# A decoder block: moments of two normalisations moved to ScalarE, two residuals to TensorE, value products paired, weights of the second stage loaded early

## What is computed

```python
x = x + self_attention(layernorm(x))                  # 3 live branches of 16 heads, windows as masks
q = split(layernorm(x) @ Wq.T + bq)                   # 16 heads of 32
k, v = split(ctx @ Wk.T + bk), split(ctx @ Wv.T + bv) # ctx: 722 keys per batch
scores = einsum('bhqd,bhkd->bhqk', q, k) / sqrt(32)
top, idx = top_k(scores, 32)                          # the 32 highest of 722, for each row
x = x + (softmax(top) @ v[idx]) @ Wo.T + bo
x = x + real(ifft(fft(layernorm(x)) @ w)) + bias      # folded into one 512x512 matrix M
```

## Time and profile before

| | us |
|---|---|
| device time, median of 3 runs (2321.08 to 2322.66) | 2322.45 |
| device time of the profiled execution | 2323.47 |
| its span | 2321.6 |
| DVE busy | 1950.9 (84%) |
| PE busy | 2076.8 (89%) |
| PEld busy | 1627.4 (70%) |
| ACT busy | 1266.3 (55%) |
| POOL busy | 1277.2 (55%) |

### The profile page before, as it was taken

How to read it: one execution, slowest core, us unless ns; L and a number is a source line. 1 busy time by engine, 2 the same in 40 slices (tenths; PEclk the granted TensorE clock), 3 DMA queues, 4 the chain that set the end, 5 groups by cost and what they waited for, 6 DMA issues and landing times. The chain is left out here.

```text
span 2321.6 us, 50944 instructions
## 1 busy us (share of the span) xinstructions
PE 2076.8 (89%) x19760; PEld 1627.4 (70%) x19760; DVE 1950.9 (84%) x3662; ACT 1266.3 (55%) x2464; POOL 1277.2 (55%) x1473
## 2 busy tenths in 40 slices
PE   2899999999957889999999999999999999999966
PEld 1566666666644778787787787887878778788754
DVE  4757676676722499999999999999999999999995
ACT  4333333333312476766666666766666766666652
POOL 2555646465641465656556656556556655665642
PEclk9999999999968899999999999999999999999977
DMA  5000000000036100000001000010000000100000
GB/s 190 12 16 20 16 23 13 23 13 26 9 82 191 30 19 13 30 26 21 18 21 38 19 20 25 13 37 18 20 26 23 28 18 21 37 18 21 8 1 11
DMA packets 41501, 70.42 MB, mean 30 GB/s; under 512 B 4639, under 2 KB 21167, under 8 KB 41261
## 3 DMA queue, kind: packets, MB, share of 16 engines
q1 hardware_dynamic: 35868, 56.31, 7.8%
q0 software_dynamic: 3632, 7.58, 1.4%
q10 hardware_dynamic: 1760, 3.28, 0.5%
HBM read 60.54 MB, written 9.86 MB: 30 GB/s over the span
## 5 line engine op out<-in xcount | busy, mean ns | idle before, releaser
L1384 DVE MATCH_REPLACE8 ca_W<-ca_top,ca_W 128x722 f32<-128x722 f32 (+1 forms) x624 | 553.1, 892 | 0.0
L1372 DVE MAX8 ca_top<-ca_W 128x8 f32<-128x722 f32 (+1 forms) x624 | 536.8, 897 | 2.2
L950 POOL TENSOR_TENSOR ca_S<-ca_S,ca_W 128x722 f32<-128x722 f32 (+1 forms) x208 | 358.6, 1743 | 270.5 <-ACT ca_W L1229 270.5
L1229 ACT ACTIVATE ca_W<-ca_W,ca_shift 128x722 f32<-128x722 f32 (+1 forms) x208 | 185.6, 892 | 83.8 <-DVE ca_W L1384 83.7
L927 POOL TENSOR_TENSOR ca_KL<-ca_K,ca_KH 128x384 fp32r<-128x384 f32 (+1 forms) x128 | 122.7, 959 | 191.5 <-ACT ca_KH L1221 189.7
L1251 ACT ACTIVATE ca_PT<-ca_pT 128x768 f32<-128x768 f32 (+1 forms) x208 | 163.4, 786 | 105.4 <-PE ca_pT L1091 105.1
L88 PE MATMUL ca_pS<-ca_KH,ca_QH 128*128 128x362 f32 (+1 forms) x384 | 149.7, 390 | 79.1 <-ACT ca_S L1246 77.4
L1124 PE MATMUL ca_pO<-ca_PT,ca_V 128*32 128x56 f32 (+5 forms) x4608 | 216.9, 225 | 0.0
L1239 ACT ACTIVATE ca_S<-ca_S,ca_shift 128x722 f32<-128x722 f32 (+1 forms) x208 | 175.8, 891 | 60.8 <-POOL ca_shift L942 60.5
L1362 DVE MAX8 ca_top<-ca_S 128x8 f32<-128x722 f32 (+1 forms) x208 | 178.9, 897 | 28.2 <-ACT ca_S L1246 27.7
L88 PE MATMUL ca_pF<-ca_cH,ca_WkH 128*128 128x338 f32 (+1 forms) x512 | 191.8, 375 | 10.2 <-POOL ca_cL L935 9.5
(11 more groups left out here) (212 smaller groups left out, 5178.0 us busy)
## 6 DMA issues: line engine op xcount, KB each, us to landing
ca_raw<-in_ctxT SPq DMA_DIRECT2D x32, 384.0 KB, 4.2
ca_raw<-in_ctxT SPq DMA_DIRECT2D x32, 338.0 KB, 3.0
sa_xin<-in_x SPq DMA_DIRECT2D x16, 200.0 KB
sa_xres<-in_x SPq DMA_DIRECT2D x16, 200.0 KB
x_scratch<-sa_x SPq DMA_DIRECT2D x16, 200.0 KB
x_scratch<-y_scratch POOLq DMA_DIRECT2D x16, 200.0 KB, 15.1
ca_xin<-x_scratch SPq DMA_DIRECT2D x16, 200.0 KB
ca_x<-x_scratch SPq DMA_DIRECT2D x16, 200.0 KB
```

Source lines behind the costliest of these rows:

```text
L950: pool.tensor_tensor(S[k][rows, :], S[k][rows, :], W[r][rows, :], ALU.subtract).then_inc(p_ready, 1)
L1229: act.activation(W[r][rows, :], W[r][rows, :], ACT.Exp, bias=shift[rows, r:r + 1], scale=SCALE).then_inc(f_ready, 1)
L1372: n_of[t.i] = order.mark(dve.max(top[r][rows, 8 * k:8 * k + 8], W[r][rows, :]))
L1384: ins = dve.match_replace(W[r][rows, :], eight, W[r][rows, :], REMOVED)
```

## The change

Six edits, in one version:

1. **Early loads.** A class `Early` places the fold matrices, the DFT matrix, the signs and the eight pieces of Wk and Wv over memory of the self program that its last batch no longer reads. SyncE issues their 29 transfers in that batch, behind a wait for the last product that reads it.
2. **Another order for batch 0.** `FIRST_PLAN` and `FIRST_SLICES` take all K slices first, and the V slices in step 0; the first score of batch 0 stands behind five slices. A second pair of context buffers (`cH0`, `cL0`) holds the second half. VectorE, idle there, makes the low parts of context and queries. The bias product (L1159 before) goes into batch 0.
3. **Six score buffers for seven**, taken round by step over the batches; the `settle` instructions (empty ones) are gone.
4. **Paired value products.** Instead of one tile's products after each transpose, the products of both tiles of a step stand at its end, from two `PT` buffers; `strip_order` orders the four blocks by how far each strip has come.
5. **Moments on ScalarE.** Total and sum of squares come from ACTIVATEs with an accumulated output, mean and scale from four small GpSimd operations, and an ACTIVATE does the scaling. BN_STATS, BN_AGGR, the epsilon and both scalings leave VectorE.
6. **Residuals on TensorE.** `x2` is multiplied with the identity into `pX` after the product, so that ScalarE only copies.

```diff
+class Early:
...
+            self.fold = {n: sb("fold_" + n, [128, CC, D]) for n in FOLDS}
+            self.dft, self.signs = sb("dft", [128, CC, D]), sb("signs", [128, CC, 4, 2])
+            self.staged = [sb(f"staged{u}", [128, D]) for u in range(2 * CC)]
...
+                    if cur and not nxt:
+                        sp.wait_ge(qk_mm, QB * B)
+                        early.load(sp)
...
-    RING, SLOTS = 4, 7
+    RING, SLOTS = 4, 6
+    FIRST_SLICES = sorted(SLICES, key=lambda x: x[1])
+    FIRST_PLAN = [([8, 9, 10], [11, 12, 13]), ([], [0, 1]), ([2], [3]), ([4], []), ([], []), ([], []), ([5, 6, 7], [])]
...
+            def mean(done):
+                pool.tensor_scalar(away[:, :], total[:, :], -1.0 / D, None, ALU.mult).then_inc(done, 1)
+
+            def scales(done):
+                order.after(order.mark(pool.tensor_scalar(rstd[:, :], squares[:, :], 1.0 / D, LN_EPS, ALU.mult, ALU.add)))
+                order.after(order.mark(pool.tensor_tensor(rstd[:, :], rstd[:, :], minus_half[:, :], ALU.pow)))
+                pool.tensor_tensor(center[:, :], away[:, :], rstd[:, :], ALU.mult).then_inc(done, 1)
...
+            def strip_order(sizes):
+                at, order = {}, []
+                for n, (strip, columns) in enumerate(sizes):
+                    for k in range(KC):
+                        order.append((at.get(strip, 0), n, k))
+                        at[strip] = at.get(strip, 0) + columns
+                return [(n, k) for _, n, k in sorted(order)]
...
-                        for c in range(CC):
-                            ins = pe.matmul(pX[0:T, :], ctxT[:, c, :], WoT[:, c, :], start=c == 0, stop=c == CC - 1)
-                        ins.then_inc(y_mm, 1)
+                        for c in range(CC):
+                            pe.matmul(pX[0:T, :], ctxT[:, c, :], WoT[:, c, :], start=c == 0, stop=False)
+                        pe.wait_ge(xb_ready, b.count(1, 0))
+                        pe.matmul(pX[0:T, :], ident[0:T, 0:T], x2[:, :], start=False, stop=True).then_inc(y_mm, 1)
...
-                        values(*old[1])
+                        values(*old)
...
+                    if s == 3 and prev:
+                        act.wait_ge(mean2_ready, b.count(1, 0))
+                        act.activation(pX[0:T, :], x2[:, :], ACT.Square, bias=away[:, 0:1],
+                                       accum_out=squares[:, 0:1]).then_inc(squares2_ready, 1)
...
+                    if s == 2 and prev:
+                        act.wait_ge(y_mm, b.count(1, 0))
+                        act.activation(x2[:, :], pX[0:T, :], ACT.Copy, accum_out=total[:, 0:1]).then_inc(x2_ready, 1)
...
-                        if k == 0 and s == 3 and prev:
-                            dve.wait_ge(y_mm, b.count(1, 0))
-                            dve.wait_ge(xb_ready, b.count(1, 0))
-                            dve.tensor_tensor(x2[:, :], pX[0:T, :], x2[:, :], ALU.add).then_inc(x2_ready, 1)
...
-                            row_stats(dve, order, x2[:, :], stats[:, :], mv[:, :], var2_ready)
```

413 lines of the change are left out of this document (239 added, 174 removed).

## The result

| | before | after |
|---|---|---|
| device time, median of 4 runs each | 2321.76 us (2319.46 to 2322.66) | 2236.81 us (2235.66 to 2242.63) |
| ratio, 95% interval | | 0.9641 (0.9622 to 0.9659) |
| profiled execution, its span | 2323.5, 2321.6 us | 2236.97, 2235.2 us |

A forecast was written before the change was run, and what follows sets the result against it. VectorE's full list was taken to bound the batches, TensorE 6% behind. Gains 72.8 + 2.6 + 47 - 1 - 3 = 118.4 us gave 2204 us, 5.1% faster; own range 2192 to 2214, with rivals 2190 to 2238.

The forecast's parts named there:

- VectorE's list: VectorE in the batches: all extras but one product leave its work, 89.0 + 0.3 us a batch for 94.5.
- The pairs: TensorE's paired value products: 1.3 us a pair for 2.05, saving 4.5 us a batch, hidden and not in the sum.
- The identity matmuls: Both residual matmuls on TensorE: 0.9 us each, 1.8 a batch, taken as hidden behind VectorE.
- The early loads: Start of the cross program: with the data there, the second product ends at 714, 21.6 us earlier.
- The end: After the last pick: residual matmuls and moments cost more, pairing saves about 1; sum 3 us more, 34 us in all.
- 85.9: TensorE's predicted time a batch in us, 88.6 + 1.8 - 4.5, under VectorE's 89.3.
- The step that failed: VectorE in the batches: period 89.3 us for 94.5 if nothing else limits; 14 x 5.2 = 72.8 us gained.
- second rival: TensorE becomes the bound if pairing saves nothing: 90.4 us a batch, 2220 us, up to 2250; chance 8%.
- first rival: A new wait in the batches, a score late for VectorE: 1 to 2.5 us a batch, 2220 to 2242; 15%.
- The start: Cross program's start: first MAX8 at 734, step 1 of batch 0 at 754 instead of 801.07, 47 us gained.
- third rival: Start shorter by less: first input needs all of `x1_scratch`, queries 10 to 15 us later, 2214 to 2219; 12%.
- up to 5 us: Self program's end: possible delay if the last batch's attention covers the late residual load too thinly.

## Why the forecast was 32 us short

The measured 2236.8 us is 23 us above the forecast's own range (2192 to 2214) and stands at the upper edge of the one with the rivals (2190 to 2238); as a ratio, 0.9641 lies just outside what 2238 makes of 2322.45, 0.9636.

**What was right.** VectorE's list: 89.05 us busy a batch for 89.0 + 0.3. The pairs:

```profile
1741.07 1.34 PE L1184 MATMUL ca_pO<-ca_PT,ca_V 128*32 128x100 f32 x47
```

They take 1.24 to 1.34 us (forecast 1.3) and save 4.6 us of TensorE a batch (4.5). The identity matmuls take 1.02 us for two records each (0.9 forecast). The early loads are worth 19.7 us (21.6 forecast for the product M). The end: 31.7 us for 34.

**Sizes that were off, without harm.** TensorE was busy 84.2 us a batch and not 85.9. ScalarE came to 67.8, under the 69 to 73 that I gave it: the seven ACTIVATEs sum to the 4.7 us forecast, but its records overlap, so that its busy time grew by 3.5. I also miscounted: the moments need four accumulator reads a batch, not three, and GpSimd got eight small operations for two, not six.

**The step that failed** is the condition in "The new period is 89.0 + 0.3 = 89.3 us for 94.5, 5.2 less, if nothing else limits", which I took as met because pairing "keeps TensorE out of the way". I compared TensorE's busy time, 85.9, with 89.3 and put its waits for ScalarE at nothing. The runs showed in its place a path through TensorE and ScalarE of 90.7 us: TensorE is busy 84.2 us a batch and waits 6.3 more, VectorE isn't on the chain, and each edit that takes something from this path (the copy's order, the identity matmul, the low clock) shortens the kernel by 10 to 15 us, while VectorE's list stays at 89.

The waits stood in the trace of before, where over the 14 batches TensorE is busy 1241.5 us and waits, with

```profile
PE ca_pS L88 <- ACT ca_S L1246: 54.1, 37, 3.5
PE ca_pO L1120 <- ACT ca_PT L1251: 15.1, 15, 1.1
PE ca_pX L1062 <- DVE ca_xin L1394: 7.2, 10, 2.0
PE ca_pF L88 <- ACT ca_K L1219: 0.4, 1, 0.4
```

76.8 us more, 5.5 a batch, all but 0.5 of it for ScalarE's answer to TensorE's own product (score, transposed weights). It is tempting to add them: 85.9 + 5.0 = 90.9, near the 90.7 measured. That this fits is luck: the first term is 1.7 too large and the second 1.3 too small. Nor could one know then that these waits would stay. Before, busy time and waits make up 94.2 of TensorE's 94.4 us although VectorE is the bound, and ScalarE, for which it waits, itself waited for VectorE:

```profile
ACT ca_W L1229 <- DVE ca_W L1384: 50.8, 44, 2.5
```

These 50.8 us (3.6 a batch) stand at the exponentials ahead of the copies. After the change there is no such wait of ScalarE in the list, and TensorE's waits are 6.3 all the same. So the waits were the term to put into the range, as a risk; their size after the change no row of before gives.

My second rival said of TensorE's gaps that they "would not all vanish", but with the condition that pairing saves nothing; pairing saved all it should, and TensorE with ScalarE set the period all the same. The first rival named the symptom, a score that comes late once a batch, at 1 to 2.5 us; the period is 1.4 longer. I had given the two 23% together. That the six score buffers caused it isn't borne out: ScalarE's copy of a score never waits for a transpose's release in the trace, only for the score. No run had seven buffers.

**The size of each part in the ring.** ScalarE's order in step 6: 10 us. The FFN's identity matmul, 0.9 us of TensorE: 14.6. The clock: 11 us with one wait filled; both filled bring it to 1.00, and with the start's share the kernel is 22 us down, of which the second filling is no part that shows in the period. These overlap and can't be added: each gives the ring slack, and VectorE's list is the floor at 89.3, at most 20 us away. I first took the ring to close over the steps 4 to 6, from VectorE's first MAX8s of step 4 through ScalarE's exponentials and back to the score. The chain doesn't bear this out: it goes through all seven steps without VectorE. No run measured its length by itself, and GpSimd's part in step 4 (the subtraction, `rZ` and `shift` ahead of ScalarE's next exponential) was not tried.

**A page that spoke for more room.** The Trainium skill, "Perfetto Trace Analysis", section "Identifying the Most-Contended Engine", judges TensorE's headroom by its share of peak FLOPs and by its weight loads, not by matmul busy time. These loads are 992.24 of 1269.68 us, so that by the second measure an estimated 22% were free, in a kernel that becomes 14.6 us faster without one matmul of 0.9 us a batch. Here the measurement decides against it: what counted was the order of work and waits on the chain, which no busy share shows.

**The start**, 9.1 us late at step 1. The third rival (all of `x1_scratch` must land first, 10 to 15 us) was right in kind and smaller: 6.4 us of the first MAX8, gone with a semaphore for batch 0's rows. The other 2.8 us are the self program's later end. I had allowed "up to 5 us" if the last loads' cover were too thin, but it wasn't the load that came late; TensorE stood still and then ran at the low clock:

```profile
633.70 0.45 PE L587 MATMUL sa_pt<-sa_rden,sa_ident 32*32 32x100 f32 x10 [2.06 <-issue]
...
641.79 5.34 PE L609 MATMUL sa_pw<-sa_WO,sa_rb 128*100 128x512 f32 x8 [0.63 <-DVE sa_rb L493]
```

Before, the second took 3.65 us. **Batch 0** had 2.6 us more of stalls than the 1 I took (0 to 5 allowed). I read this as TensorE having no room beside its V slices; the one other order that I tried for three K slices gained nothing.

## What to carry to other kernels

Before an edit shortens the busiest engine's list, look at the second one's waits for answers to its own products. If its busy time and these waits together come above the new list, the gain may end there, whatever the busy share says: take that into the range, but as a risk and not as a sum. The waits are no constant: they were 4.5 us a batch with the pairs undone, 6.3 in the change and 8.0 with the moments back on VectorE. In a ring look first for work that stands on the answering engine ahead of the answer (here four exponentials ahead of a copy), and move it only where nothing else waits behind: the same move in all steps but one cost 33 us against the move in step 6 alone. Work that was shifted to the second engine because it had room (an identity matmul of 0.9 us to spare 0.67) must be weighed again after all other edits.
